# Four-layer window transformer on one core: probabilities turned in five pieces, heads in four row groups, values spread through DRAM, arrays laid out as the tiles

## What is computed

```python
qkv = (xw @ qkv_w + qkv_b).reshape(b, n, 3, NUM_HEADS, hd).transpose(2, 0, 3, 1, 4)
q, k, v = (qkv[0], qkv[1], qkv[2])
attn = jnp.einsum('bhnd,bhmd->bhnm', q * hd ** (-0.5), k) + bias + mask
attn = jax.nn.softmax(attn, axis=-1)
out = jnp.einsum('bhnm,bhmd->bhnd', attn, v).transpose(0, 2, 1, 3).reshape(b, n, c)
x = shortcut + window_reverse(out @ proj_w + proj_b)
x = x + gelu(norm(x) @ mlp_w1 + mlp_b1) @ mlp_w2 + mlp_b2
```

## Time and profile before

| | us |
|---|---|
| three runs | 8,497.1; 8,497.35; 8,511.64 |
| median | 8,497.35 |
| profiled execution, time and span | 8,497.1 |
| TensorE busy | 7,930.6 (93%) |
| VectorE busy | 6,104.5 (72%) |
| GpSimd busy | 5,402.6 (64%) |
| ScalarE busy | 5,155.3 (61%) |

### The profile page before, as it was taken

How to read it: one execution, slowest core, us unless ns; L and a number is a source line. 1 busy time by engine, 2 the same in 40 slices (tenths; PEclk the granted TensorE clock), 3 DMA queues, 4 the chain that set the end, 5 groups by cost and what they waited for, 6 DMA issues and landing times.

```text
span 8497.1 us, 316211 instructions
## 1 busy us (share of the span) xinstructions
PE 7930.6 (93%) x111222; PEld 5968.4 (70%) x111222; DVE 6104.5 (72%) x18304; ACT 5155.3 (61%) x9130; POOL 5402.6 (64%) x6733
## 2 busy tenths in 40 slices
PE   2999999999999999999999999999999999999997
PEld 1777777777777777776767777777776777777766
DVE  3777767767777776776777677776677767777666
ACT  1755747646774664755767476574577647566456
POOL 6865646556785665655778465564678756566565
PEclk9999999999999999999999999999999999999998
DMA  3100010000011011000001101000101100000001
GB/s 42 22 13 10 15 27 15 10 12 13 10 21 31 13 20 23 15 7 16 9 15 21 28 15 28 15 15 4 20 3 21 26 21 15 6 14 13 7 17 23
DMA packets 597322, 142.33 MB, mean 17 GB/s; under 512 B 596066, under 2 KB 596662, under 8 KB 596877
## 3 DMA queue, kind: packets, MB, share of 16 engines
q1 hardware_dynamic: 574508, 131.49, 7.8%
q10 hardware_dynamic: 16865, 3.97, 0.3%
q0 software_dynamic: 5504, 1.21, 0.1%
HBM read 31.76 MB, written 19.27 MB: 6 GB/s over the span
## 4 chain that ended last, share of the span: by engine, by line
PE 70%; DVE 12%; issue 8%; ACT 3%; DVEq 3%; POOL 1%; POOLq 0%; ACTq 0%
PE ps L912 12%; PE ps L973 11%; PE ps L900 8%; PE ps L876 7%; PE ps L1016 7%; PE ps L989 7%; PE ps L919 5%; PE ps L942 3%; PE ps L952 3%; DVE bst L1042 3%; ACT PT L779 3%; PE ps L961 2%; DVE xn L1195 2%; PE ps L856 2%; DVE S L1244 2%
## 5 line engine op out<-in xcount | busy, mean ns | idle before, releaser
L643 POOL TENSOR_TENSOR S<-S,mx 113x588 f32<-113x588 f32 (+1 forms) x2048 | 2065.4, 1008 | 1528.3 <-DVE mx L1246 1524.5
L779 ACT ACTIVATE PT<-ps 98x588 f32<-98x588 f32 (+1 forms) x2048 | 1182.5, 577 | 1239.9 <-PE ps L973 1233.1
L912 PEld LDWEIGHTS ps<-Vbd,PT 98*49 98x49 f32 x40960 | 1113.0, 125 | 666.4 <-issue 642.7
L1244 DVE TENSOR_TENSOR S<-ps,bias 113x588 f32<-113x588 f32 (+1 forms) x1536 | 962.9, 627 | 856.7 <-PE ps L900 856.7
L912 PE MATMUL ps<-Vbd,PT 98*49 98x18 f32 (+1 forms) x40960 | 1326.7, 202 | 171.7 <-ACT PT L779 109.7
L1246 DVE TENSOR_REDUCE mx<-S 113x12 f32<-113x588 f32 (+1 forms) x2048 | 1359.6, 664 | 70.5
L973 PEld LDWEIGHTS ps<-ident,S 113*98 113x98 f32 x10240 | 1040.6, 128 | 473.1 <-issue 382.0
L973 PE MATMUL ps<-ident,S 113*98 113x113 f32 x10240 | 1346.0, 262 | 3.8 <-ACT S L761 3.4
L761 ACT ACTIVATE S<-S 113x588 f32<-113x588 f32 (+1 forms) x2048 | 1240.0, 605 | 54.4 <-POOL S L643 52.3
L989 PEld LDWEIGHTS ps<-w,G 128*98 128x98 f32 x12288 | 1151.1, 168 | 161.6 <-issue 89.5
L989 PE MATMUL ps<-w,G 128*98 128x96 f32 (+1 forms) x12288 | 1152.0, 250 | 0.8 <-DVE x L1329 0.8
(11 more groups left out here) (104 smaller groups left out, 10493.0 us busy)
## 6 DMA issues: line engine op xcount, KB each, us to landing
Vbd<-Vd SPq DMA_DIRECT2D x1536, 41.3 KB
Vbd<-Vd SPq DMA_DIRECT2D x512, 38.3 KB
mask<-L_conv_mask_matrix_dram SPq DMA_DIRECT2D x258, 37.5 KB
x<-x_dram SPq DMA_DIRECT2D x48, 84.0 KB
out_dram<-x SPq DMA_DIRECT2D x48, 84.0 KB
x<-x_dram SPq DMA_DIRECT2D x228, 10.5 KB
out_dram<-x SPq DMA_DIRECT2D x228, 10.5 KB
out_dram<-x SPq DMA_DIRECT2D x180, 18.4 KB
```

Source lines behind the costliest of these rows:

```text
L643: pool.tensor_tensor(v, v, m, ALU.subtract).then_inc(a_sub, 1)
L779: act.activation(PT[:, (s + 3) % 4, 0:blocks, :, :].rearrange("p (b t) w n -> p b (t w) n", b=banks), PTps[:, PT_BANK[l] - 3:PT_BANK[l] - ...
L912: last = pe.matmul(Ops[ROW2 * w:ROW2 * w + N, p, b, :].rearrange("p (a n) -> p a n", a=2), PT[:, p, b, w, :], v, start=True, stop=True)
L1244: dve.tensor_tensor(dst, scores, b, ALU.add).then_inc(a_bi, 1)
```

## The change

Six things are changed, all in layers 0 to 2 unless stated:

- **Heads in four row groups.** The query and key weights are padded to 4 x 32 columns, three heads in each group of 32. QK has eight matmuls per pair of 3 x 49 columns in place of six of 4 x 49; `key_slot` runs three times per quad in place of four, on 128 partitions in place of 96.
- **Probabilities in five pieces.** They are turned in pieces of 123, 122, 123, 122 and 98 keys, so a piece can end inside a head. The identity is replaced by a permuted one, `turn`, that puts the 98 real queries first; five pieces fit one PSUM bank, and `PT` is copied as 123 x 490.
- **PV in five matmuls per window**, of 27, 27, 27, 27 and 18 columns; the second of each couple accumulates onto the head that both share. The loop over the windows is now outside, that over the pieces inside (for layer 3 as well).
- **Values through DRAM.** `Vd` is ordered by head. SyncE writes it to a DRAM tensor in one DMA, waits for that, and reads six pieces back into `Va` and `Vb` (two into `Vl` in layer 3).
- **Arrays in the tiles' layout.** Images, mask, weights and bias tables are given to the program as the tiles need them, and the output is taken in that form. A group's tokens are four DMAs, the weights some fifteen.
- **Fills.** The memsets of padded tiles move from GpSimd to VectorE, ahead of its first statistics; the masked bias tables take 12 additions on 128 partitions in place of 26 on 49.

```diff
-KEYROW = 4 * N
+KEYROW = 3 * N
...
+KEYS_A, KEYS_B = 2 * N + 25, 2 * N + 24
+WIDE_A, WIDE_B = 3 * QUAD * 9, 2 * QUAD * 9
...
+    row = np.arange(P) % GRP
+    c["kmask"] = ((row // 8)[:, None] == np.arange(3)[None]).astype(np.float32)
+    tokens = [*range(N), *range(ROW2, TOK), *range(N, ROW2)]
+    c["turn"] = np.eye(TOK, dtype=np.float32)[:, tokens]
...
+        def blocks_of(nh, par, w):
+
+            if nh == 4:
+                v = Vl[:, par, w, :, :].rearrange("p a (m j n) -> p a m j n", m=2, j=QUAD)
+                return [(PAIR, PAIR * m, 2 * m, v[:, :, m]) for m in range(2)]
+            va = Va[:, par, w, :, :].rearrange("p a (m j n) -> p a m j n", m=3, j=QUAD)
+            vb = Vb[:, par, w, :, :].rearrange("p a (m j n) -> p a m j n", m=2, j=QUAD)
+            out = []
+            for m in range(2):
+                out.append((KEYS_A, 5 * N * m, 5 * m, va[:, :, m]))
+                out.append((KEYS_B, 5 * N * m + KEYS_A, 5 * m + 2, vb[:, :, m]))
+            out.append((PAIR, 10 * N, 10, va[0:PAIR, 0:2, 2]))
+            return out
...
         def tokens(eng, g, store, s, first=0, last=IMGS, turn=0, turns=1):
...
+                at = slice(image * PAIRS_IMG, (image + 1) * PAIRS_IMG)
+                far = dram[g, :, at.start * C:at.stop * C]
...
                             par = (j + 1) % 2
-                            for w in range(2):
+                            wide = QUAD * (C + nh)
+                            sp.dma_start(vs[par, :, 0:wide], Vd[:, 0:wide]).then_inc(s_vw, 16)
+                            written = ((i + 1).index + g * LAYER_QUADS + l * NQ + 1) * 16
+                            sp.wait_ge(s_vw, written if i.static else sp.snap(written))
...
-                                    sp.dma_start(Vbd[N * a:N * (a + 1), par, :, w, a, 0:width],
-                                                 Vd[N * w:N * (w + 1), :, a, 0:width]).then_inc(s_vb[par], 16)
...
+                                for c in range(2):
+                                    part(Va[N * c:N * (c + 1), par, :, c, :], 0, N, c * WIDE_A, WIDE_A)
+                                part(Va[2 * N:KEYS_A, par, :, 2, 0:WIDE_B], 0, 25, 2 * WIDE_A, WIDE_B)
+                                part(Vb[0:24, par, :, 0, :], 25, N, 2 * WIDE_A, WIDE_B)
...
-                        if s == 3 and nh == 12 and on(1):
-                            key_slot(3).then_inc(a_ke, 1)
...
-                            for k in range(3 if nh == 12 else 4):
+                            for k in range(4):
...
-                            for b in range(blocks):
-                                for w in range(2):
-                                    v = values_of(Vbd[:, o if s < 3 else t, p, w, :, :], nh, b)
-                                    last = pe.matmul(Ops[ROW2 * w:ROW2 * w + N, p, b, :].rearrange("p (a n) -> p a n", a=2),
-                                                     PT[:, p, b, w, :], v, start=True, stop=True)
+                            for w in range(2):
+                                for b, (rows, _, h, v) in enumerate(blocks_of(nh, o if s < 3 else t, w)):
+                                    v = v[:, :, p]
+                                    out = Ops[ROW2 * w:ROW2 * w + N, p, h:h + v.shape[1], :]
+                                    last = pe.matmul(out, PT[0:rows, p, b, N * w:N * (w + 1)], v,
+                                                     start=(nh == 4 or b % 2 == 0), stop=True, skip_group_check=True)
...
-                            for b in range(blocks):
-                                at = PTps[:, PT_BANK[l] - 3 + b // 3, 2 * (b % 3):2 * (b % 3) + 2, :]
-                                last = pe.transpose(at.rearrange("p w q -> p (w q)")[:, 0:TOK],
-                                                    S[:, e, PAIR * b:PAIR * (b + 1)], ident[0:TOK, 0:TOK])
+                            for b, (rows, at, _, _) in enumerate(blocks_of(nh, 0, 0)):
+                                last = pe.transpose(ps[0:rows, PT_BANK, PAIR * b:PAIR * b + TOK],
+                                                    S[:, e, at:at + rows], turn[:, :])
```

More of the change, by code:

```diff
@@ L392, in waits @@
             return wait
[L395 to L406, removed]
-                    for w in range(2):
[L408 to L414, removed]
         def tokens(eng, g, store, s, first=0, last=IMGS, turn=0, turns=1):
             dram = out if store else x_in
-            rows_of = x[:, bass.ds((g % 2) * NP, NP), :].rearrange("p (a j) c -> p a j c", j=4)
-            for n, (q, a, j, row, col) in enumerate(runs(first, last)):
-                if n % turns != turn:
+            for image in range(first, last):
+                if image % turns != turn:
                     continue
[L423 to L427, removed]
+                at = slice(image * PAIRS_IMG, (image + 1) * PAIRS_IMG)
+                far = dram[g, :, at.start * C:at.stop * C]
+                near = x[:, (g % 2) * NP + at.start:(g % 2) * NP + at.stop, :].rearrange("p a c -> p (a c)")
                 dst, src = (far, near) if store else (near, far)
@@ L432, in mask_quad @@
             for w in range(2):
[L433 to L440, removed]
+                at = (g * NP + q * QUAD) * N
+                src = d["mask"][w, :, bass.ds(at, QUAD * N)]
+                sp.dma_start(mask0[ROW2 * w:ROW2 * w + N, slot, :, :].rearrange("p a b -> p (a b)"), src).then_inc(s_mask[slot], 16)
+        TOK_DMAS = IMGS
+        HALF_DMAS = IMGS // 2
+        n_const = [0]
         def load(eng, dst, src):
@@ L444, in load @@
             n_const[0] += 16
[L446 to L473, removed]
-        def stage(l):
[L476 to L483, removed]
-                staged = stage(l)[WS * r:WS * (r + 1), :].rearrange("p (h a b) -> p h a b", h=nh, a=WS)
-                for rk in range(WS):
-                    src = bass.AP(d[names(l)["table"]].tensor, (r + rk) * TABLE,
-                                  [[1, WS], [TABLE * TABLE, nh], [1, WS]])
-                    eng.dma_start(staged[:, :, rk, :], src).then_inc(loaded, 16)
+        STAGED = sum(HEADS[1:]) * N
+        def stage(l):
+            return room[:, sum(HEADS[1:l]) * N:sum(HEADS[1:l + 1]) * N]
         @block.sync
@@ L568, in _ @@
             pool.memset(neghalf[:], -0.5).then_inc(s_memset, 1)
[L569 to L579 removed]
+            pool.wait_ge(s_memset, 2)
             def layer(l, g):
@@ L1070, in load_stats @@
                     keep(i - 1, (i - 1).index * QUAD, QUAD, (j + 1) % 2, x_agg, x_mv)
+            dve.memset(mask0[:], 0.0).then_inc(s_maskpad, 1)
+            for t in (hT, OT, h4):
+                dve.memset(t[:], 1.0)
+            for t in (Va, Vb, Vl):
+                last = dve.memset(t[:], 0.0)
+            last.then_inc(s_memset, 1)
             dve.wait_ge(s_x0, 16 * HALF_DMAS)
```

255 lines of the change are left out of this document (140 added, 115 removed).

## The result

| | before | after |
|---|---|---|
| median of four runs, us | 8,501.19 (8,497.1 to 8,511.64) | 8,392.34 (8,389.86 to 8,394.56) |
| ratio, 95% interval | | 0.9871 (0.9857 to 0.9885) |
| profiled execution, span | 8,497.1 | 8,390.0 |

The change is faster by 109 us, 1.3%, well clear of the spread of the runs. The forecast was 233 us. Its sign was right and its size was not: less than half came. The two profiled executions differ by 107.1 us, and the trace shows where they lie.

What follows compares the result with a forecast made beforehand. TensorE, busy 93% of the span, was taken to bound the kernel, with savings showing only in stretch B. 8497.1 - 127 (quads) - 79 (start) - 27 (end) = 8264 us; forecast's own range 8180 to 8400, with rivals to 8710.

Steps and rivals of the forecast that it cites:

- side by side: PV, layers 0 to 2: both windows' passes run at once on their array halves; 0.60 us for 0.66, 0.06 saved.
- its own sign of being wrong: The forecast is wrong if TensorE's time for PV grows, or stretch A grows although its work is less.
- stretch B: Quad from slot 3's PV to next slot 1's PV, 5.86 us, no TensorE wait worth naming; 0.33 saved per quad.
- Stretch A: Quad from slot 1's PV to slot 3's PV, 5.59 us, ended by VectorE; nothing gained, idle time 0.33 to 0.66.
- QK and projections: TensorE groups: QK 0.42 us, 0.07 saved; queries' and keys' projections 0.03 longer each, one in each stretch.
- Start: Before the first copy of values: loads at 160 GB/s, that copy at about 95 for 173.89; 79 us saved, at best 87.
- End: Last stores: 2.4 MB at 160 GB/s, 17 us for 44.6; 27 us saved, ends 4 and 35.
- Values through DRAM, ScalarE: DRAM chain of 8.3 to 11.1 us fits the 11.07 available; ScalarE's savings hide behind TensorE; both costed at nothing.
- Rival three: Attention quads: fewer, larger pieces bring nothing, quads stay at 11.45 us, only start and end gain; 8391 us, chance 0.13.
- Rival one: PV's windows run one after the other, PV 1.00 us; 8690 us, slower; chance 0.31, partial forms included.
- partial form: PV with a queue of some entries: a time between the forecast's and rival one's; counted within the 0.31.
- turning point: PV time from which the whole kernel is slower than before: about 0.85 us, six tenths of the way.

Runs made afterwards that it cites:

- windows inside: The changed kernel with PV's two loops swapped back, pieces outside and windows inside, so the two windows' matmuls alternate: 8,194.02 us, 0.9636 of before.
- kernel before with windows outside: The kernel before with only PV's loops swapped, twelve passes of one window ahead of twelve of the other: 8,892.63 us, one run.
- the statistics moved: Changed kernel with windows inside, TensorE's register work placed ahead of its waits in the source, and VectorE's token statistics moved from slot 1 to slot 3: 8,170.09 us.
- the split loads: The changed kernel with each of its three 97-row weight loads issued as 96 rows and one row: 8,370.59 us.

## Why the prediction was partly wrong

- **PV: the step that failed.** "I take side by side", 0.60. It is 0.86, between the two ends of 0.575 and 1.00 that the text had worked out, and its own sign of being wrong, that PV grows, came. The reading of QK was right as far as it went: passes of different tiles do overtake each other, and here the second window's first pass starts ahead of three of the first's. The Trainium skill ("TensorE: Matmul & The Clock Gate", Part 3) states that matmuls start and end strictly in program order. These rows do not agree with it. But QK has two passes for each tile, six tiles deep. No pass there goes ahead of more than five others, so its rows do not speak "as far as ten passes", and of any one tile only a single pass is overtaken: that says nothing on how many passes of one tile may wait. The text itself saw that "no row shows a tile's passes overtaking more than two of another tile" and still took the end, not the middle. The price is the difference between two runs: 198 us.
- **The size, had PV been side by side.** The run with windows inside is the forecast's own case, 8,194 for 8,264. In its layers 1 and 2 stretch B is 0.41 shorter, where 0.33 was forecast: PV fell by 0.09 where 0.06 was taken, B's turnings by 0.09 and 0.07 where 0.05 was. Stretch A is 0.08 shorter, where nothing was forecast. With 0.49 a quad there and 0.39 in layer 0 the quads give 175 us for 127, start and end 103 for 106. The rest of the 70, some 25 us, lies between the layers and was not forecast.
- **QK and projections.** 0.43 for 0.42; keys 0.03 longer as said. The queries' read 0.05 shorter and not longer, but some 0.07 of their 0.81 before was waiting ahead of the turning. In the kernel before with windows outside they are 0.74, and 0.76 is 0.03 more than that, as said.
- **Stretch A.** It was said to stay at 5.59. It went from 5.62 to 5.55 on the average. Its TensorE work had grown, so that idle time before slot 3's PV fell from 0.37 to 0.24; it did not grow to 0.66. With windows inside, where TensorE's work in A is less, A is 5.54 and TensorE waits 0.70 in it: 0.40 before slot 3's PV and 0.30 before the turnings. That time saved in A only becomes idle time was thus right. That VectorE alone ends it was taken from one row, `Ot`, which ended 0.24 before the wait did; with the statistics moved A is 5.61, and the waits stand before the turnings, for the exponential.
- **Start.** 68 for 79. The images came faster than the 160 GB/s worked out from a share (252), the statistics ended at 59.5 (62 said). But the weights did not land beside them: 18.6 us of waiting for constants, which the split loads removed. With those the first copy comes at 88.6, a gain of 85, where the text's best end was 87.
- **End.** 35 for 27: the last stores move 241 GB/s where 160 was taken.
- **Values through DRAM, ScalarE.** Nothing, as said.
- **The rivals.** Rival three named 8,391 and the time is 8,392, but by luck, not by its mechanism: QK and the turning gave 0.72 a quad, and PV took it back. Rival one in its partial form is what happened, and the time it gives is not slower: its turning point, PV at about 0.85, was set with 106 us of gain at the ends counted in; with a measured 0.86 the quads alone stand at +0.06. The point was too low because the turning's gain was undersized, stretch A shrank a little, and layer 3's PV, priced at up to 65 us, cost next to nothing.

## What to carry to other kernels

When small matmuls go to the two column halves of the array, write them in turns, at most two matmuls (four passes of 32-bit floats) for one half at a time; with three and more in a row for one half the other started late in every run here. Where a trace shows some overlap, count how deep it goes for one part of the array before it is used for a longer row. A load with a prime number of rows, 97 here, is cut in two.

## What was not expected of the hardware

- Three passes of 32-bit floats (or one whole matmul behind the one under way) wait for a half of the array, and the next stops the ones behind it for the other half: second window at the seventh of ten, at the ninth of twelve, at the third of six, at once with four.
- With loads of 97 rows under way the DMA share is 0.07 (25 GB/s); with each as 96 and 1 rows it reaches 0.90 (207 GB/s).
- A register operation on TensorE that stands behind a wait: in quads with it slot 3's QK with its wait lasts 0.19 longer than in quads without (0.76, 0.57). That was only seen, not tried.
